# Three of sixteen output tiles finished by ScalarE and an adding DMA of GpSimd's queue

## The reference, cut to what matters

```python
x = x + gru(cond, x, W_ih, W_hh, b_ih, b_hh)          # 64 steps, one after the other
# second layer, for every sequence b:
block_repr = x.reshape(B, 8, 8, H).sum(axis=2)
keys = normalise(block_repr @ Wk.T) * rms_weight
attended = softmax(keys @ q) @ block_repr              # one vector per sequence
y = x + (attended @ Wo.T)
x = x + (y - mean(y)) / sqrt(var(y) + 1e-6) * gamma + beta
```

## Time and profile before

| | |
|---|---|
| time, median of 3 runs | 375.47 us (374.59 to 376.02) |
| the profiled execution's own time | 376.31 us |
| its span in the trace | 374.2 us |
| TensorE / VectorE / ScalarE / GpSimd busy | 97% / 71% / 42% / 4% of the span |
| last `add_gcp` matmul ends | 370.08 us |
| last `finish` begins, takes | 370.83 us, 0.74 us |
| last store issued | 371.60 us |

### The profile page before, as it was taken

How to read it: one execution, slowest core, us unless ns; L and a number is a source line. 1 busy time by engine, 2 the same in 40 slices (tenths; PEclk the granted TensorE clock), 3 DMA queues, 4 the chain that set the end, 5 groups by cost and what they waited for, 6 DMA issues and landing times.

```text
span 374.2 us, 9793 instructions
## 1 busy us (share of the span) xinstructions
PE 362.1 (97%) x3267; PEld 212.2 (57%) x3267; DVE 264.3 (71%) x1138; ACT 158.6 (42%) x506; POOL 15.3 (4%) x47
## 2 busy tenths in 40 slices
PE   8899999999999999999999999999999999997895
PEld 5355555666665556666555666655566666334672
DVE  2746667777676778686768767676778676768897
ACT  3501326262534344352626262534344364756510
POOL 5013000000000000000000000000000000100000
PEclk9999999999999999999999999999999999998999
DMA  7985544323232322324141323232322322110038
GB/s 269 403 322 159 165 102 151 103 68 102 72 98 70 93 68 56 98 59 109 44 106 40 98 70 98 70 98 70 78 75 65 97 56 72 49 45 16 17 138 312
DMA packets 28100, 40.05 MB, mean 107 GB/s; under 512 B 3120, under 2 KB 19120, under 8 KB 28080
## 3 DMA queue, kind: packets, MB, share of 16 engines
q1 hardware_dynamic: 28080, 39.79, 36.5%
HBM read 19.60 MB, written 4.19 MB: 64 GB/s over the span
## 4 chain that ended last, share of the span: by engine, by line
PE 86%; DMA 5%; DVE 4%; SPq 1%; ACT 1%; issue 1%; DVEq 0%
PE gates_ps L601 43%; PE gi_ps L570 36%; DMA gcx<-in_w_ih_dram 3%; DMA w_hh<-in_w_hh_dram 2%; PE third_ps L601 1%; PE keys_ps L601 1%; PE fourth_ps L601 1%; PE keys_ps L711 1%; SPq L268 1%; PE first_ps L730 1%; DMA h_tok<-hist 1%; SPq L259 1%; PE keys_ps L678 1%; PE gi_ps L671 1%; PE gi_ps L583 1%
## 5 line engine op out<-in xcount | busy, mean ns | idle before, releaser
L601 PE MATMUL gates_ps<-w_hh,turned 128*32 128x384 f32 x1920 | 167.3, 489 | 0.5 <-DVE turned L805 0.5
L601 PEld LDWEIGHTS gates_ps<-w_hh,turned 128*32 128x32 f32 x1920 | 56.5, 109 | 85.5 <-issue 56.4
L570 PE MATMUL gi_ps<-w_ih_hi,xt_hi 128*128 128x384 f32 x240 | 86.8, 364 | 0.0
L570 PE MATMUL gi_ps<-w_ih_hi,xt_lo 128*128 128x384 f32 x240 | 80.7, 338 | 0.0
L570 PE MATMUL gi_ps<-w_ih_lo,xt_hi 128*128 128x384 f32 x240 | 79.7, 334 | 0.0
L460 ACT ACTIVATE rz<-gates_ps 128x256 f32<-128x256 f32 x60 | 23.1, 385 | 128.7 <-PE gates_ps L601 128.6
L869 DVE TENSOR_TENSOR rz<-gates_ps,rz 128x128 f32<-128x128 f32 x60 | 17.5, 291 | 79.4 <-ACT rz L460 79.4
L570 PEld LDWEIGHTS gi_ps<-w_ih_hi,xt_hi 128*128 128x128 f32 x240 | 44.9, 187 | 37.5 <-issue 36.8
L570 PEld LDWEIGHTS gi_ps<-w_ih_lo,xt_hi 128*128 128x128 f32 x240 | 45.1, 188 | 0.0
L570 PEld LDWEIGHTS gi_ps<-w_ih_hi,xt_lo 128*128 128x128 f32 x240 | 44.9, 187 | 0.0
L805 DVE STREAM_TRANSPOSE turned<-hist 128x32 f32<-128x32 f32 (+1 forms) x192 | 36.7, 216 | 2.2
(11 more groups left out here) (209 smaller groups left out, 294.6 us busy)
## 6 DMA issues: line engine op xcount, KB each, us to landing
gi<-gi_tok SPq DMA_DIRECT2D x60, 192.0 KB, 3.4
x1t<-in_x_t_dram SPq DMA_DIRECT2D x16, 256.0 KB, 3.2
gcx<-in_x_tok_dram SPq DMA_DIRECT2D x16, 256.0 KB, 3.2
h_tok<-hist SPq DMA_DIRECT2D x64, 64.0 KB, 2.2
out_dram<-gcx SPq DMA_DIRECT2D x16, 256.0 KB, 2.3
gcx<-in_w_ih_dram SPq DMA_DIRECT2D x4, 768.0 KB, 8.5
w_hh<-in_w_hh_dram SPq DMA_DIRECT2D x4, 768.0 KB, 9.0
wo_t<-in_wo_t_dram SPq DMA_DIRECT2D x1, 1024.0 KB, 5.7
```

Source lines behind the costliest of these rows:

```text
L570: mm = pe.matmul(gi_ps[tok][:, 0:G3], a[:, k, :], w[:, k, gi_cols(j)], start=(m == 0), stop=(m == 3 * NJ - 1))
L601: mm = pe.matmul(gates_bank(t)[j * B:(j + 1) * B, P:], before[:, k * B:(k + 1) * B], chunk(w_hh, k, j), start=False, stop=(k == NJ - 1), s ...
```

## The change

Quads 5, 7 and 10 are no longer finished by VectorE. The two parts of their result are not added on an engine. ScalarE multiplies `gcx` of the quad by rstd in place and copies the bank to SBUF (`laid_kept`), SyncE stores the first part with the plain store that the quad had before, and once this has landed, an adding transfer on GpSimd's own DMA queue adds the second part onto it in HBM. The bank of such a quad is free once ScalarE has copied it. The program now ends when 13 stores, the three plain stores of the scaled quads and the three adding transfers have landed.

```diff
--- before.py
+++ after.py
@@ -109,6 +109,8 @@
         out_ps = [first_ps[0], third_ps, small_ps, gi_ps[1], gates_ps, gi_ps[0]]
         cross_ps = [keys_ps, gi_ps[0], keys_ps]
         parts_i = [(0,), (1,), (2, 3)]
+        added_quads = (5, 7, 10)
+        laid_kept = [end[:, (28 + 4 * m) * P:(32 + 4 * m) * P] for m in range(len(added_quads))]
 
         w_ih_in = [sem(f"w_ih_in{k}") for k in range(NJ)]
         w_hh_in = [sem(f"w_hh_in{k}") for k in range(NJ)]
@@ -155,6 +157,8 @@
         var_ready, std_ready, rstd_ready, rstd_spread, rstd_laid, rstd_kept = (
             sem("var_ready"), sem("std_ready"), sem("rstd_ready"), sem("rstd_spread"), sem("rstd_laid"), sem("rstd_kept"))
         u_laid, out_ready, out_stored = sem("u_laid"), sem("out_ready"), sem("out_stored")
+        scaled_ready, laid_copied, laid_stored = sem("scaled_ready"), sem("laid_copied"), sem("laid_stored")
+        scaled_stored = [sem(f"scaled_stored{m}") for m in range(len(added_quads))]
 
         def wait(eng, s, value):
 
@@ -188,6 +192,14 @@
         def column(tile, quad):
 
             return tile[:, quad:quad + 1] if isinstance(quad, int) else tile[:, bass.ds(quad, 1)]
+
+        def dve_outs(quad):
+
+            return quad + 1 - added_outs(quad)
+
+        def added_outs(quad):
+
+            return sum(q <= quad for q in added_quads)
 
         def spread_rstd(eng, part):
 
@@ -307,10 +319,18 @@
                 sp.dma_start(h_tok[:, j * P:(j + 1) * P], hist[j * B:(j + 1) * B, Q:S, :]).then_inc(h_tok_in, 16)
             for quad in range(NQ):
 
-                sp.wait_ge(out_ready, quad + 1)
-                sp.dma_start(out[:, quad, :], gcx[:, quad, :]).then_inc(out_stored, 16)
-
-            sp.wait_ge(out_stored, 16 * NQ)
+                if quad in added_quads:
+                    sp.wait_ge(scaled_ready, added_outs(quad))
+                    sp.dma_start(out[:, quad, :], gcx[:, quad, :]
+                                 ).then_inc(scaled_stored[added_outs(quad) - 1], 16)
+                else:
+                    sp.wait_ge(out_ready, dve_outs(quad))
+                    sp.dma_start(out[:, quad, :], gcx[:, quad, :]).then_inc(out_stored, 16)
+
+            sp.wait_ge(out_stored, 16 * (NQ - len(added_quads)))
+            for stored in scaled_stored:
+                sp.wait_ge(stored, 16)
+            sp.wait_ge(laid_stored, 16 * len(added_quads))
 
         @block.gpsimd
         def _(pool):
@@ -365,6 +385,11 @@
             pool.tensor_tensor(key_rms[:], key_ss[:], half[:, 0:2], ALU.pow).then_inc(key_rms_ready, 1)
             pool.wait_ge(last_var_ready, 1)
             pool.tensor_tensor(last_rms, last_var, half[:, 0:1], ALU.pow).then_inc(last_rms_ready, 1)
+            for m, quad in enumerate(added_quads):
+                pool.wait_ge(laid_copied, m + 1)
+                pool.wait_ge(scaled_stored[m], 16)
+                pool.dma_start(out[:, quad, :], laid_kept[m], accum_op=ALU.add).then_inc(laid_stored, 16)
+
         @block.scalar
         def _(act):
             def split_x(quad):
@@ -548,7 +573,21 @@
             move_s2(NQ - Q, Q, fourth_ps, 4 * Q)
             keep_rstd(1)
             root(2)
+
+            def scale_and_copy(quad):
+
+                m = added_quads.index(quad)
+                act.wait_ge(gcx_ready, quad + 1)
+                act.wait_ge(rstd_kept, (1, 2, 3, 3)[quad // Q])
+                act.activation(gcx[:, quad, :], gcx[:, quad, :], ACT.Copy, scale=rstd_tok[:, quad:quad + 1]
+                               ).then_inc(scaled_ready, 1)
+                act.wait_ge(u_laid, quad + 1)
+                act.activation(laid_kept[m], out_ps[quad % len(out_ps)][:], ACT.Copy).then_inc(laid_copied, 1)
+
+            scale_and_copy(added_quads[0])
+            scale_and_copy(added_quads[1])
             keep_rstd(2)
+            scale_and_copy(added_quads[2])
 
         @block.tensor
         def _(pe):
@@ -660,8 +699,10 @@
                 bank = out_ps[quad % len(out_ps)]
                 if quad == NQ - 1:
                     pe.wait_ge(x1t_ready, NQ)
-                if quad >= len(out_ps):
-                    pe.wait_ge(out_ready, quad - len(out_ps) + 1)
+                if quad - len(out_ps) in added_quads:
+                    pe.wait_ge(laid_copied, added_outs(quad - len(out_ps)))
+                elif quad >= len(out_ps):
+                    pe.wait_ge(out_ready, dve_outs(quad - len(out_ps)))
                 elif bank is gates_ps:
                     pe.wait_ge(gcp_kept, 1)
                 elif bank is cross_ps[1]:
@@ -1119,10 +1160,12 @@
             inverse(2)
             spread_rstd(dve, 2)
             for quad in range(Q, 2 * Q):
-                finish(quad)
+                if quad not in added_quads:
+                    finish(quad)
             centre_tokens(NQ - 1)
             for quad in range(2 * Q, NQ):
-                finish(quad)
+                if quad not in added_quads:
+                    finish(quad)
 
 
 def kernel(**inputs):
```

## The result

The changed kernel takes 379.65 us (median of 4 runs, 379.16 to 380.06) against 375.75 us for the kernel before in the same comparison. The medians differ by 3.9 us. The ratio is 1.0113, with a 95% interval from 1.0087 to 1.0139: 4.2 us or 1.1% slower. I had forecast 3.1 us.

The account below looks back on a forecast made before the run. TensorE and VectorE reach the last finishes together, with DMA engines full. Gain 0, ScalarE's cost 0, adds about 3.1 us: 375.47 + 3.1 = 378.6 us, 0.8% slower; range 376.0 to 382.5, likeliest case 377.3 to 380.5.

Parts of the forecast that it names:

- Gain on the path 0: Output's end: three finishes less free 2.0 us of VectorE, but finish 14 still waits for TensorE's last matmul; gain 0.
- ScalarE's cost 0: ScalarE after root(2): six instructions of 0.63 to 0.67 us fit, keep_rstd(2)'s slip to 364.5 is covered; cost 0.
- DMA engines full, so added transfers push the end: Last stores, 366 to 373 us: DMA engines always busy, three adds overflow by 1.2 to 3.3 us.
- Room of 0.8 us: DMA engines from 364.3 to 373.3 us: 9.0 us hold 8.2 us of stores, leaving 0.8 us free for adds.
- Engine time 0.68 to 1.36 us for an add: DMA engines: an add costs between a store's 0.68 us and 1.36 us for two reads per write; high price taken.
- Landing 2.3 to 5.5 us: GpSimd's queue: an add lands after 2.3 us if like a store, 5.5 us if a load and then a store.
- the prediction's two ways: Kernel's end: DMA overflow, 3.3 us, and latency of the last add, 2.9 us, agree on about 3 us.
- Signs: Trace after: finish 14 still near 370.2, HBM reads up 0.8 MB, span ending with landing of quad 10's add.
- C: TensorE waiting for VectorE's banks: relief makes it faster, 373.5 us, shown by finish 14 before 369.5; chance 0.04.
- B: GpSimd's queue much dearer, adds one after another: 388 us, half of it 381 to 382; chance 0.18.
- The estimate of 2.6 us: GpSimd's queue: plain transfer at 2.0 us plus bytes over 436 GB/s; last add would land near 373.4, hidden.
- Rival A: Adds cheap, 0.68 us of engine time, landing in 2.3 to 3 us: 375.5 to 377.2 us; chance 0.28 including no change.

Follow-up runs that it names:

- e2: Changed kernel without GpSimd's three second transfers; scale, copy and plain store stay: 375.00 us against 375.09, ratio 1.0004.
- e9: Changed kernel with only quad 5 split, its second transfer a plain store on ScalarE's queue: 376.17 us against 375.25, ratio 1.0028.
- e4: Changed kernel with three plain second transfers on ScalarE's queue in place of GpSimd's adding ones: 376.99 us, ratio 1.0062.
- e1: Changed kernel with GpSimd's three second transfers plain instead of adding: 377.50 us against 375.09, ratio 1.0072.
- e3: Changed kernel with only quad 5 split, one adding transfer: 377.39 us against 375.09, ratio 1.0060.
- e5: Changed kernel with only quad 10 split, one adding transfer: 377.32 us, ratio 1.0059.
- e12: Changed kernel with only quad 1 split instead of 5, 7 and 10, one early adding transfer: 376.98 us, ratio 1.0039.
- e6: Changed kernel with quads 1, 2 and 3 split instead of 5, 7 and 10, three earlier adding transfers: 378.36 us, ratio 1.0084.
- e7: Changed kernel with the three adds waiting for all plain stores and each for the one before it: 390.77 us, one run.
- e8: Changed kernel without second transfers and with quads 5, 7 and 10 not stored at all, 13 stores: ratio 0.9991.
- e10: Changed kernel with GpSimd adding the parts in SBUF and one plain store writing each sum: 376.30 us against 375.34, ratio 1.0013.

## Why the prediction was right, and where a size was off

- *Gain on the path 0.* Right. e2 (1.0004) shows it, and the waits of 1.30 and 0.67 us show where the 2.0 us of VectorE went.
- *ScalarE's cost 0.* Right, by e2, with 0.71 and 0.60 us for what I took as 0.63 and 0.67. keep_rstd(2) slipped by 0.2 us (362.36 + 1.83 = 364.19, against 363.96 before), not to 364.5. In the same place the prediction prices a slip from 363.96 to 364.5 at 0.7 us; it is 0.5.
- *DMA engines full, so added transfers push the end.* Right. e9 (0.70 us of engine time, 0.8 us of tail), e4 (2.1 and 2.1), e1 (2.1 and 2.2), e3 (2.3 and 2.4) and the changed kernel (4.5 and 4.5) lie on one line. Three runs lie off it: e5 (1.7 and 2.4), where the chain of the last add ends later than the stores, and the early adds of e12 (1.8 and 0.9) and e6 (5.4 and 3.1), which use the gaps.
- *Room of 0.8 us.* Wrong: about none, and the larger of the two mis-sized terms. A plain transfer of 0.70 us should have fitted into it, but cost 0.8 in e9. The gap lies before 366 us, and no second transfer could start before 367.8 on the clock of before (365.93 + 1.83): the first scaled store took 3.3 us to land where I had taken 2.3, and the add was issued 0.7 us after that.
- *Engine time 0.68 to 1.36 us for an add.* The other mis-sized term. It measured 1.5 us (three among stores) to 2.3 us (the single one of e3), above my upper bound, so that two reads for one write is not the price. In the sum, 3 x 1.5 - 0 = 4.5 stands in place of 3 x 1.36 - 0.8 = 3.3. Of these 1.2 us the room is 0.8 and the engine time 0.4. It is as much as the miss between 3.1 and 4.2 us.
- *Landing 2.3 to 5.5 us.* Measured 5.9 to 7.1 in the changed kernel, and 4.1 to 4.4 alone. The bound left out the queueing. The issue, 0.85 to 1.08 us, was inside 0.34 to 1.18, and the store of quad 10 was issued at 365.98 + 1.83 = 367.8 and landed at 370.5, as worked out. That the prediction's two ways agreed on about 3 us was no check: the 5 us to landing in the second were chosen from a range of 2.3 to 5.5, and both ways came out too low.
- *Signs.* The last landing is that of the last plain store and of the last add together, at 376.4 and 376.3, and not of the add alone. By the letter the sign of C came true, finish 14 began at 368.34 and so before 369.5; but the whole stretch stood 1.83 us earlier, and 0.09 us behind TensorE's last matmul (367.66 + 0.59 = 368.25) is where it stood before. The HBM reads did not grow. The range's upper end, 382.5, is also a little above the half of B, 381 to 382, that it is said to be.
- What the Trainium skill (DMA: Bandwidth & Descriptors, "Issuing engines are not separate DMA queues") says is borne out by e1 and e4: the tail grew by 2.2 and 2.1 us, whichever queue issued. The estimate of 2.6 us by the same page of the Trainium skill ("Anatomy of one DMA") was met by no transfer here: plain ones of GpSimd's queue took 3.6 to 4.7 us among stores (e1), adding ones 4.1 to 4.4 us alone (e7). No run has a plain one alone, for which it might hold.
- Rival A fell with the engine time. B's serial queue did not come: the second add was issued at 367.1, the first landed at 365.9 + 5.9 = 371.8. C (TensorE waiting for banks) was refuted by e2.

What stays open: why one add took 2.3 us of the engines and each of three 1.5. No run here changes what a packet of an add waits for. The last store's issue was also slow in the changed kernel (1.47 us against 0.34), and how much of its 6.5 us to landing that explains was not separated from the rest.

## What to carry to other kernels

Before moving work off an engine, ask whether another one releases the same last step at the same time; here TensorE, VectorE and the DMA engines all reached it within 0.2 us of each other, and relief of one was worth nothing. A second transfer in place of an instruction pays its engine time in full wherever the DMA engines are already full, and stores that are late there stay late. In an earlier gap it can still delay the end, as in e12, where the mean share had caught up and one or two of the 16 engines had not. And before two traces are compared by their clocks, find where they part: here 1.83 us lay ahead of the change. Price an adding transfer from a run by itself, not as a store: it took 2.1 us of the 16 engines for 256 KB, where a plain one took 0.70.

## What I had not expected of the hardware

- An adding transfer of 256 KB to HBM takes two to three times a plain one's engine time (1.5 to 2.3 us against 0.70), with a DMA share over 1.0 at as little as 51 GB/s.
- It does not show in the row for HBM reads: 19.60 MB both before and after.
- SyncE's issue of a store can be slow: up to 1.56 us in e6 and 1.47 us at the end of the changed kernel, against 0.34 us. In these two runs many transfers were under way; but single issues took 1.2 us in the kernel before and 1.5 us in e2 as well, without adds.
- A `tensor_tensor` of 128 x 512 fp32 on GpSimd took 1.27 to 1.5 us beside VectorE's finishes, and was hidden.
- TensorE's granted clock from 345 to 350 us was 0.66 to 0.74 in the profiled executions of the kernel before, e7, e8 and e10, and 1.00 in the ten others. Between the traces of before and after, this stretch is worth 1.3 us, more than several of the effects measured here. No run shows what sets it.
